# Message stage of a graph network: one transpose of each gathered row instead of two, with the edge's scalar moved into the radial layer

## The reference, cut to what matters

```python
s = s @ W_up_s * inv                     # scalars of a node, 32 channels
v = einsum('nui,uw->nwi', v, W_up_v)*inv # vectors of a node, 32 channels x 3
h = silu(silu(edge_feats @ A1 + b1) @ A2 + b2)     # radial network, 64 wide
w0, w1, w2, w3 = split(h @ A3, 4)        # 4 x 32 weights of each edge
y_s, y_v = edge_attrs[:, :1], edge_attrs[:, 1:4]
out_s0 = s[sender] * y_s * w0
out_s3 = einsum('eui,ei->eu', v[sender], y_v) / R3 * w3
out_v1 = s[sender][:, :, None] * y_v[:, None, :] * w1[:, :, None]
out_v2 = v[sender] * y_s[:, :, None] * w2[:, :, None]
message = segment_sum(concat(...), receiver) / 10.0
out_s = message_s @ W_out_s ; out_v = message_v @ W_out_v   # then a layer norm
```

## Time and profile before

| | |
|---|---|
| runs | 3766.24, 3753.16, 3766.95 us; median 3766.24 us |
| span of the profiled execution | 4163.4 us |
| profiled execution beside the median | 397.2 us (10.5%) longer; no other time of it is given |
| granted TensorE clock in it, mean | 0.735 |
| busy: PE, DVE, ACT, POOL | 2637.4, 1800.3, 1103.2, 2178.9 us |
| message stage | 2990 to 3684 us of the span |
| update stages | 1290 to 1414 and 2526 to 2651 us |

### The profile page before, as it was taken

How to read it: one execution, slowest core, us unless ns; L and a number is a source line. 1 busy time by engine, 2 the same in 40 slices (tenths; PEclk the granted TensorE clock), 3 DMA queues, 4 the chain that set the end, 5 groups by cost and what they waited for, 6 DMA issues and landing times. The chain is left out here.

```text
span 4163.4 us, 41911 instructions
## 1 busy us (share of the span) xinstructions
PE 2637.4 (63%) x11696; PEld 1689.0 (41%) x11696; DVE 1800.3 (43%) x4207; ACT 1103.2 (26%) x2880; POOL 2178.9 (52%) x1937
## 2 busy tenths in 40 slices
PE   1547973665563648964555564359667786759696
PEld 1324653454452335643444442234323343334343
DVE  6433433554453544434444453320246685650203
ACT  0113430222232614421222233410224453430001
POOL 4357556666675757566666675620156577520000
PEclk9965555777776865556766777679778897869797
DMA  9997996777774549996777773537245564527372
GB/s 314 364 291 279 395 338 183 234 227 232 218 206 118 95 148 332 394 311 180 219 232 220 222 185 89 152 98 282 92 125 147 141 180 136 140 73 292 114 288 100
DMA packets 672304, 872.83 MB, mean 210 GB/s; under 512 B 136977, under 2 KB 557144, under 8 KB 631524
## 3 DMA queue, kind: packets, MB, share of 16 engines
q1 hardware_dynamic: 314324, 581.00, 39.8%
q0 software_dynamic: 118784, 157.05, 16.1%
q10 hardware_dynamic: 239008, 132.59, 10.8%
HBM read 441.21 MB, written 429.28 MB: 209 GB/s over the span
## 5 line engine op out<-in xcount | busy, mean ns | idle before, releaser
L1716 POOL DMA_INDIRECT att_rows<-table,kvrow x784 | 796.0, 1015 | 400.9 <-issue 230.3
L1484 POOL DMA_INDIRECT matrix<-count,place x392 | 621.5, 1585 | 279.2 <-DMA matrix<-count,place 196.9
L2119 POOL DMA_INDIRECT msg_rows<-rows,msg_src x392 | 411.4, 1050 | 448.6 <-DMA msg_src<-in_src_pt 218.1
L1774 PE MATMUL att_po<-att_message,att_mate 128*128 128x264 f32 (+1 forms) x1568 | 438.3, 419 | 300.0 <-issue 199.4
L1774 PEld LDWEIGHTS att_po<-att_message,att_mate 128*128 128x128 f32 x1568 | 296.1, 232 | 400.6 <-issue 324.9
L1607 PE MATMUL tab_bank<-wk,tab_kv 32*128 32x256 f32 x1600 | 378.6, 686 | 74.3 <-DVE tab_part L1566 43.3
L1566 DVE COPY tab_part<-tab_bank 128x512 f32<-128x512 f32 x400 | 258.2, 686 | 357.6 <-DMA table<-tab_part 249.5
L1842 ACT ACTIVATE att_out<-att_po 128x136 f32<-128x136 f32 (+1 forms) x784 | 230.0, 337 | 456.1 <-remote 241.6
L1607 PE MATMUL tab_bank<-wv,tab_kv 32*128 32x256 f32 x1600 | 332.4, 613 | 0.0
L1591 ACT ACTIVATE tab_part<-tab_bank 128x512 f32<-128x512 f32 x400 | 222.4, 594 | 367.5 <-DMA table<-tab_part 267.6
L1900 DVE TENSOR_TENSOR att_prod<-att_rows,att_pq 128x512 f32<-128x512 f32 x196 | 133.6, 682 | 419.5 <-issue 400.1
(11 more groups left out here) (399 smaller groups left out, 3970.2 us busy)
## 6 DMA issues: line engine op xcount, KB each, us to landing
table<-tab_part SPq DMA_DIRECT2D x200, 1024.0 KB
gsum_cells<-matrix SPq DMA_DIRECT2D x50, 1604.0 KB
att_sums<-att_out ACTq DMA_DIRECT2D x196, 272.0 KB
matrix<-a SPq DMA_DIRECT2D x25, 1604.0 KB
nb_cells<-matrix SPq DMA_DIRECT2D x25, 1604.0 KB
a<-query_rows SPq DMA_DIRECT2D x144, 256.0 KB
query_rows<-a SPq DMA_DIRECT2D x16, 1568.0 KB
att_message<-in_ea_rows SPq DMA_DIRECT2D x98, 256.0 KB
```

Source lines behind the costliest of these rows:

```text
L1484: nc.gpsimd.indirect_dma_start(D.matrix, bass.IndirectOffsetOnAxis(ap=K.place[:, col:col + 1], axis=0), K.count[:, col:col + 1], None, com ...
L1716: nc.gpsimd.indirect_dma_start(rows[g % RR][:, j, :], None, D.table, bass.IndirectOffsetOnAxis(ap=K.kvrow[:, t:t + 1], axis=0)).then_inc(r ...
L1774: nc.tensor.matmul(po[j][:, 0:w], mate[h % RS][:, j, :], message[h % RM][:, j, 0:w], start=True, stop=True).then_inc(summed, 1)
L2119: nc.gpsimd.indirect_dma_start(rows[g % RR][:, j, :], None, D.rows, bass.IndirectOffsetOnAxis(ap=src[:, t:t + 1], axis=0)).then_inc(rows_i ...
```

## The change

In `messages` the gathered rows are turned once, as they are. ACT's `dim` and DVE's `scale` are gone, and so is the table `edge`. PE's `turn(g)` waits for the gather itself and makes four transposes into `pu[g % 2]`; ACT makes one copy, `up`, from a ring of three. The scalar attribute is put into the radial layer: `update` multiplies `h2` by it (DVE, `dim_pair`, once a pair, with the scalar broadcast over 64 partitions by two transfers) and stores the product as a second DRAM tensor `lit`. `weigh` reads its upper half from `lit` and its lower half from `hidden`. The components are multiplied in after the turn: DVE's `take_side(g)` makes `side` = `up` x `axes`, and `axes` is also what `vec` uses in place of `out_y`. `axes` comes from an input that already holds each component 32 times, 96 rows. `pback` becomes two tiles. On PE the turn is one group further ahead; on SP the load of `axes` stands before the loads of the radial layer; POOL waits for `turned` alone.

```diff
 # update
+            def load_scalar(i):
+                for n2 in range(2):
+                    g = 2 * (pairs.start + i) + n2
+                    sp.dma_start(scalar[i % 4][n2 * 64:n2 * 64 + 64, :],
+                                 D.scalar[g * W:(g + 1) * W].partition_broadcast(64)).then_inc(scalar_in[i % 4], 16)
+            for i in range(4):
+                load_scalar(i)
             for i in range(many):
                 v = pairs.start + i
                 sp.wait_ge(lit2, i + 1)
                 sp.dma_start(D.hidden[:, v * W:(v + 1) * W], h2[i % 4][:, :]).then_inc(hid_out[i % 4], 16)
+                sp.wait_ge(dimmed, i + 1)
+                sp.dma_start(D.lit[:, v * W:(v + 1) * W], dim[i % 4][:, :]).then_inc(lit_out[i % 4], 16)
+                if i + 4 < many:
+                    load_scalar(i + 4)
...
             def second_layer(i):
                 act.wait_ge(hid2, i + 1)
                 if i >= 4:
                     act.wait_ge(hid_out[i % 4], 16 * (i // 4))
+                    act.wait_ge(dimmed, i - 3)
...
+            def dim_pair(i):
+                dve.wait_ge(lit2, i + 1)
+                dve.wait_ge(scalar_in[i % 4], 32 * (i // 4 + 1))
+                if i >= 4:
+                    dve.wait_ge(lit_out[i % 4], 16 * (i // 4))
+                nc.vector.tensor_tensor(dim[i % 4][:, :], h2[i % 4][:, :], scalar[i % 4][:, :], ALU.mult).then_inc(dimmed, 1)
...
                 if k + 2 < n:
                     scale(k + 2)
+                if k >= 1:
+                    for i in radial_pairs(k - 1):
+                        if i >= 1:
+                            dim_pair(i - 1)
...
 # messages
             def turn(g):
-                for n, ready in enumerate((dimmed, scaled)):
-                    pe.wait_ge(ready, g + 1)
-                    if g >= 1:
-                        pe.wait_ge(upcopied, 2 * g + n - 1)
-                    for j in range(J):
-                        last = nc.tensor.transpose(pu[n][:, j * P:(j + 1) * P], sc[g % 2][n][:, j, :], K.ident[:, :])
-                    last.then_inc(turned, 1)
+                pe.wait_ge(rows_in[g % RR], 16 * J * (g // RR + 1))
+                if g >= 2:
+                    pe.wait_ge(upcopied, g - 1)
+                for j in range(J):
+                    last = nc.tensor.transpose(pu[g % 2][:, j * P:(j + 1) * P], rows[g % RR][:, j, :], K.ident[:, :])
+                last.then_inc(turned, 1)
...
-                for n in range(2):
-                    act.wait_ge(turned, 2 * g + n + 1)
-                    if g >= 2:
-                        act.wait_ge(multiplied, 2 * (g - 2) + n + 1)
-                    nc.scalar.activation(un[g % 2][n][:, :], pu[n][:, :], ACT.Copy).then_inc(upcopied, 1)
+                act.wait_ge(turned, g + 1)
+                if g >= RU:
+                    act.wait_ge(multiplied, 2 * (g - RU) + 1)
+                    act.wait_ge(sided, g - RU + 1)
+                nc.scalar.activation(up[g % RU][:, :], pu[g % 2][:, :], ACT.Copy).then_inc(upcopied, 1)
...
+            def take_side(g):
+                dve.wait_ge(upcopied, g + 1)
+                dve.wait_ge(axes_in[g % RS], 16 * (g // RS + 1))
                 if g >= 2:
-                    dve.wait_ge(turned, 2 * (g - 1))
-                nc.vector.tensor_tensor(sc[g % 2][1][:, :, :].rearrange("p j (b c) -> p j b c", c=32),
-                                        rows[g % RR][:, :, :].rearrange("p j (b c) -> p j b c", c=32),
-                                        edge[:, g, :, 1:5].unsqueeze(3).broadcast_to([P, J, 4, 32]), ALU.mult).then_inc(scaled, 1)
+                    dve.wait_ge(multiplied, 2 * (g - 1))
+                nc.vector.tensor_tensor(side[g % 2][:, :], up[g % RU][:, :], axes[g % RS][:, :], ALU.mult).then_inc(sided, 1)
...
-                if g + 3 < G:
-                    scale(g + 3)
+                if g + 2 < G:
+                    take_side(g + 2)
```

More of the change, by code:

```diff
@@ L677, in update @@
         turned_in = [s.sem(f"turned_in{k}") for k in range(STREAMS)]
-        hid_out = [s.sem(f"hid_out{v}") for v in range(4)]
+        hid_out, lit_out, scalar_in = ([s.sem(f"{x}{v}") for v in range(4)] for x in ("hid_out", "lit_out", "scalar_in"))
+        dimmed = s.sem("dimmed")
         a1 = s.sb("a1", [P, STACK, P])
@@ L683, in update @@
         h1 = [s.sb(f"h1{v}", [P, W]) for v in range(R)]
-        h2 = [s.sb(f"h2{v}", [P, W]) for v in range(4)]
+        h2, dim, scalar = ([s.sb(f"{x}{v}", [P, W]) for v in range(4)] for x in ("h2", "dim", "scalar"))
         ph1 = [s.ps(f"ph1{v}") for v in range(R)]
@@ L2072, in messages @@
         src = s.sb("src", [P, TILES], I32)
-        edge = s.sb("edge", [P, G, J, 5])
         rows = [s.sb(f"rows{k}", [P, J, P]) for k in range(RR)]
         hidden = [s.sb(f"hidden{k}", [P, W]) for k in range(RS)]
-        out_y = [s.sb(f"out_y{k}", [P, W]) for k in range(RS)]
-        sc = [[s.sb(f"sc{u}{k}", [P, J, P]) for k in range(2)] for u in range(2)]
-        un = [[s.sb(f"un{u}{k}", [P, W]) for k in range(2)] for u in range(2)]
+        axes = [s.sb(f"axes{k}", [P, W]) for k in range(RS)]
+        up = [s.sb(f"up{k}", [P, W]) for k in range(RU)]
+        side = [s.sb(f"side{k}", [P, W]) for k in range(2)]
         prod = [s.sb(f"prod{k}", [P, W]) for k in range(2)]
@@ L2086, in messages @@
         pm = [s.ps(f"pm{k}") for k in range(2)]
-        pback = s.ps("pback")
+        pback = [s.ps(f"pback{k}") for k in range(2)]
         sums = D.sums.rearrange("(g j p) d -> g p j d", j=J, p=P)
@@ L2101, in _ @@
                 if g >= RS:
+                    sp.wait_ge(graded, g - RS + 1)
+                sp.dma_start(axes[k][32:P, :], D.axes[:, g * W:(g + 1) * W]).then_inc(axes_in[k], 16)
+                if g >= RS:
                     sp.wait_ge(radial, 2 * (g - RS + 1))
-                for n in range(2):
+                for n, half in enumerate((D.lit, D.hidden)):
                     sp.dma_start(hidden[k][n * 64:n * 64 + 64, :],
[L2105 to L2108, removed]
+                                 half[g % 2 * 64:g % 2 * 64 + 64, g // 2 * W:(g // 2 + 1) * W]).then_inc(hidden_in[k], 16)
         @block.gpsimd
@@ L2114, in _ @@
                 if g >= RR:
-                    pool.wait_ge(dimmed, g - RR + 1)
-                    pool.wait_ge(scaled, g - RR + 1)
+                    pool.wait_ge(turned, g - RR + 1)
                 for j in range(J):
@@ L2239, in _ @@
                     dve.wait_ge(added, g)
-                nc.vector.tensor_tensor(vec[:, :], pm[1][:, :], out_y[g % RS][:, :], ALU.mult).then_inc(graded, 1)
+                nc.vector.tensor_tensor(vec[:, :], pm[1][:, :], axes[g % RS][:, :], ALU.mult).then_inc(graded, 1)
                 if g + 1 < G:
@@ L2280, in build @@
     D.h_slots = dram("h_slots", (SLOTS * P, P))
-    D.hidden = dram("hidden", (P, EP // 2))
+    D.hidden, D.lit = (dram(x, (P, EP // 2)) for x in ("hidden", "lit"))
     K = Names()
```

72 lines of the change are left out of this document (28 added, 44 removed).

## The result

| kernel | runs, median | against before |
|---|---|---|
| before (beside after) | 3759.8 us | |
| after | 3792.51 us (3783.78 to 3807.26, 4 runs) | 1.0089 [1.0068, 1.0111] |

A forecast was written before the change was run, and what follows sets the result against it. The prediction took PE to bound a steady message group, with DVE 0.28 us behind. Its terms, -29 transposes, -1 start and end, 0 transfers, +5 updates, gave -25 us: 3741 us from 3766.2, own range 3715 to 3755, over all cases 3675 to 3790.

The forecast's parts named there:

- the first term: Message stage: halving PE's transposes frees 57.4 us, of which 29 us are gained before DVE takes over as bound.
- Rival A: Message stage: POOL's gathers bound it at 490 to 592 us, PE's saving is worthless; about 3769 us, chance 0.27.
- the 111 us of ring waits: Message stage: POOL's waits for ring slots, all that faster consumers could give back; counted against gathers as bound.
- the rule on operands in SBUF: DVE operations with two SBUF inputs and GpSimd operations reading SBUF exclude each other; gathers gain nothing from this change.
- +5 with bounds of 0 and 34: Both update stages: added cost of `dim_pair`, its waits and transfers, +5 us together, between 0 and +34.
- 1 us a step: Updates: allowance for ACT's `second_layer` waiting for `dimmed` of four pairs back, 1 us a step.
- with DMA at about half load: Updates: SP issues 98 broadcasts and 49 stores more, with DMA only about half loaded.
- POOL's part: Updates: POOL's scatters slowed beside DVE, 49 operations at 0 to 0.26 us, 0 to 13 us over both stages.
- POOL closes the stage and absorbs a delay: Updates: POOL still scatters for 8 us after DVE's last operation, which absorbs ACT's delay in the first update.
- rival D: Updates: all 34 us of `dim_pair` show as ACT waits each step, gathers bounding `messages`; 3800 us, chance 0.08.
- if POOL's waits vanished and the stage still stood near 600 us (A): Message stage: sign that the forecast is wrong and the gathers bound the stage.
- Rival C: Message stage: PE's idle time lowers its granted clock; at 20% more slow groups +49 us, 3815 us, chance 0.08.

The follow-up runs named there:

- the second: Repeat profile of the unchanged kernel before, no edit: 3769.66 us, message stage 551.5 us.
- e5: Kernel after, with `total` in a PSUM bank and `take_side` reading `pu` in PSUM instead of ACT's copy: 3743.9 us, 0.9958 of before.
- e2: Kernel before with only the changed message stage, both halves of the radial layer from `hidden`, scalar left out: 3774.2 us, 1.0039 of before.
- e1: Kernel before with only the changed updates; message stage as before, not reading `lit`: 3775.4 us, 1.0041 of before.
- e9: e1 with rings of four, scalar broadcasts stopped after the first four pairs of each update: 3761.3 us, 1.0012 of before.
- e10: Kernel after, with each group's four transposes made twice into the same tile: 3784.7 us, 1.0074 of before.

## Why the prediction was wrong

*The step that failed* is the first term, "57.4 x 0.28 / 0.55 = 29 us", with its premise that PE bounds a group. In the stretch in which a group took 4.54 us PE and DVE caught up: they used up rows that POOL had laid into the ring while they stood. In an ordinary execution the gathers bound the whole stage. In the first profile DVE stood for long in that stage, before `vec` above all:

```profile
DVE msg_vec L2240 <- issue: 175.2, 43, 27.1
```

In the second all waits before `vec` sum to 12 us. What made the engines stand in the first isn't known.

Rival A had it right, with the right arithmetic (490 us at best; e5's gathers take 489 from first to last). The counter-argument, the 111 us of ring waits, was a feature of that one execution. The profiled span was 10% over the runs; I had written that waits in it might not exist in the runs, and yet carried the sum over.

*In place of -29* the message stage measured +8 in the profiles, 14 in the runs of e2: the gathers met the scan at a worse moment. The prediction had the rule on operands in SBUF and drew from it that the gathers gain nothing, which held; it did not see that the overlap in time, and so the loss, can shift when nothing about the operands changes.

*The updates* were put at +5 with bounds of 0 and 34; +20 were measured in the profiles, 15 in the runs of e1. The reason given for the bound was nearly the true one (ACT waits for `dimmed` four pairs back), but the price of 1 us a step was a guess, and SP's order was left out: `hidden` stands behind `lit`. The 98 broadcasts and 49 stores were put at nothing, "with DMA at about half load"; they took it from 0.53 to 0.77, and without the broadcasts e9's chains are 9 and 19 us shorter than e1's. POOL's part was right: its scatters take 2.3 us more in the two updates, of 0 to 13. That POOL closes the stage and absorbs a delay was right too, for 14.7 and 16.8 us; the delay was 19 and 33. The outcome is rival D in kind (3800 forecast, 3792.5 measured), with 20 us in place of its 34, and the gathers' 8 us added, which D didn't have; that the totals lie so close is luck.

*Right in detail*: less of PE for the transposes, though 44 us and not 57 (eight that overlap are busy for 1.16 us a group, four for 0.72), `take_side` at 669 ns against `scale`'s 685, nothing from the transfers of `messages`. The condition "if POOL's waits vanished and the stage still stood near 600 us (A)" is what came, at 559.

*Rival C*: the granted clock of the stage, a mean over its levels of 1.2 and 2.4 GHz, fell from 0.95 to 0.92 and the `pm` matmul went from 609 to 655 ns, but PE had 140 us to spare. With twice the transposes (e10) it was 0.96, and the stage 3 us shorter, which is less than the 6 us that its gathers lose less. No time can be seen to hang on it.

Open: why the gathers meet the scan earlier in after, what share of the updates' 20 us is SP's order alone, and what slowed the first profile.

## What to carry to other kernels

Before costing work taken from an engine, add up the busy and issue time of the engine that feeds the stage: 392 x 1.25 to 1.37 us was the whole stage here but for 20 to 27 us, in every profile that matched the runs. Profile again when the profiled span is far from the median; its steady stretches can be catch-up. A ring that crosses three engines and a store queue needs room for the slowest landing in the round. That a store should not be queued behind one that becomes ready later is read from the timeline alone; no run tests it.

## What was not expected of the hardware

The lock between DVE and POOL acts by the instant. A gather that begins while a DVE operation with two SBUF inputs runs ends 0.75 us (scan) or 0.82 us (tensor_tensor) after that operation, where that is later than its own 0.944 us; if it begins before, it takes its 0.944 us, and the scan isn't held up: 77 scans of after began during a gather and took 1.27 us, as the 21 others. So in these traces the exclusion works one way. One such operand moved to PSUM and the wait is zero. In before these waits cost 41 us, more than the 29 that the prediction hoped to gain.
